# First unit of a fused state-space and feed-forward kernel: the order of the copies of the first two groups of channels, and the first product with B in quarters

## The chip, the cores and the metric

The kernel runs on one core of one Trainium2 chip. The metric is the device time of one launch in microseconds (us). The kernel before was timed three times: 323.78, 324.98 and 325.20 us, median 324.98 us.

## The reference

The input x is 4 sequences of 1024 positions with D = 128 channels, in float32. The part that matters here is the first half of a layer, a selective state-space block:

```
u  = silu(conv3(x))                       # three taps along the sequence, per channel
B, C = split(u @ W_bc + b_bc)             # 16 states each
dt = softplus((u @ W_dt + b_dt) @ W_dtp + b_dtp)
h[t, d, n] = exp(A[d, n] * dt[t, d]) * h[t-1, d, n] + B[t, n] * u'[t, d] * dt[t, d]
y[t, d]    = sum over n of C[t, n] * h[t, d, n]
x1 = layernorm(x + y + x * Dcoeff)
```

where u' is the block's own input x. The second half is a gated feed-forward layer (128 to 352 to 128) whose operands are rounded block by block to a 4-bit format, followed by another residual and layernorm. The recurrence over t is the part with most work: 128 channels by 16 states by 4096 positions.

## The kernel before

**Tiles.** The 4096 positions are cut into 8 units of 512. A unit has 128 channels x 16 states = 2048 rows of recurrence, which are handled as 16 groups of 128 partitions. A group is 32 channels (`E`) times 4 states: group k belongs to the set of states m = k // 4 and to the quarter of the channels c = k % 4. So the first four groups of a unit are the four quarters of the channels for the first set of states.

**Data of a unit.** `dtx[:, 0]` holds dt and `dtx[:, 1]` holds dt times x, with channels on the 128 partitions. Since a group has each of its 32 channels four times, once for each state, `dt_rep[:, c]` must hold quarter c of `dtx` four times over, on partitions 0-31, 32-63, 64-95 and 96-127. That is done by DMA: 4 copies of 128 KB for each quarter, 16 copies for a unit. Each quarter has its own semaphore `dt_in[c]`, complete at 64.

**Engines in the scan.** For each group ACT computes the decay `exp(A dt)` from `dt_rep[:, c, 0]` into one of three PSUM banks `ps_decay` (`decay`, L567; mean about 0.69 us). DVE multiplies `B + bias` (broadcast by PE into the bank `ps_b`, `spread_b`, L1523) with `dt_rep[:, c, 1]` into `db` (`times_b`, L1156, four quarters at once), and then runs the recurrence for a group as one scan (`scan`, L1167). POOL multiplies pairs of states with C (`times_c`, L896), and PE sums over states. C is brought onto all partitions by a PE product that ACT evacuates with a bias into `c_rep`. The engines run ahead of each other by written-out slots: step k of a unit holds decay k + 2 on ACT, scan k on DVE, the product of a pair on POOL at odd k, and pieces of the next and the previous units. A decay needs the bank that the scan of three groups before has read.

**The first unit.** It has its own head, since nothing runs beside it. `ACT` computes dt (L594), `DVE` multiplies it with x (L1133) and then prepares the quantisation of the feed-forward weights. When `dtx` is complete, ACT issues the four copies of quarter 1 (L598) and SP those of quarters 0, 2 and 3 (`replicate`, L508, called at L536). Then ACT evacuates C of set 0 (`c_of_first(0)`), loads the table set of exp and ln, evacuates C of set 1, computes decays 0 and 1 and evacuates C of set 2. PE makes each of these C products in the bank `ps_y` and may start the next one only when ACT has evacuated the one before (`c_of_first`, L1448), so the two engines take turns. After that the loop over k begins. In its first step ACT does decay 2, C of set 3, and the evacuation of the next unit's transposed x (`x_of`, L626); in its second decay 3. PE's order there is: transposes of the next unit's x, C product of set 3, the first convolution tap of the next unit (which needs `x_of`), and then `spread_b` of set 1, which needs that the product of set 0 with B is complete (`db_done`), and the other two taps.

The first product with B is made on DVE in two halves (`half_times_b`, L1146): quarters 0 and 1 in one instruction, which waits for the copies of both; then scans 0 and 1; then quarters 2 and 3 in a second instruction, then scans 2 and 3; then the product for set 1 (`times_b(s, 1, p)`, called in slot 4).

The functions that the diff touches and their callers:

Of the kernel before, what the change touches and what calls it, by code (L numbers as in the profile page):

```python
# [38 lines left out]
STATES = 4  # L39
# [145 lines left out]
def over(t, n):  # L185

    return t.rearrange("p (a t) -> p a t", a=1).broadcast_to([t.shape[0], n, t.shape[1]])


def build(nc, x, conv_w, w_bc, b_bc, w_dt, b_dt, w_dtp, b_dtp, a_log, dcoeff, w_gate, w_up, w_down, out):  # L190
# [6 lines left out]
    with ctx:  # L197
# [8 lines left out]
        def sem(name):  # L206
            return ctx.enter_context(nc.semaphore(name))
# [169 lines left out]
        conv_done = sem("conv_done")  # L377
        head_c = sem("head_c")
        head_c_done = sem("head_c_done")
        db_half = sem("db_half")  # L380
        w_magic_done = sem("w_magic_done")
        w_code_order = sem("w_code_order")
        selectors = sem("selectors")
# [82 lines left out]
        @block.sync  # L466
        def _(sp):
            def load(a, o):
                unit = a.at(1)
                if a.beyond(2):  # L470
                    sp.wait_ge(prep_mm, a.at(PREP_MM, 1 - 2 * PREP_MM))
                sp.dma_start(x_tok[o][:], x_tiles[bass.ds(unit, 1)].rearrange("a p q d -> (a p) q d"))\
                  .then_inc(x_in[o], 16)

            def load_halo(a, o):

                row = a.at(UNIT, -1 if o else UNIT)
                if a.beyond(2):
                    sp.wait_ge(sum_done, a.at(SETS, 1 - 2 * SETS))
                halo = x_feat[1][:, 0:1] if o else x_feat[0][:, UNIT + 1:UNIT + 2]  # L480
                sp.dma_start(halo, x_rows[:, bass.ds(row, 1)]).then_inc(halo_in[o], 16)

            load(Unit(0), 0)
            sp.dma_start(taps[:], conv_w.rearrange("k d -> d k")).then_inc(taps_in, 16)
            load_halo(Unit(0), 0)
            for dst, src in (
                (wdt_t, w_dt.rearrange("d r -> r d")), (wdtp, w_dtp),
                (bdt[:], b_dt.rearrange("(p a) -> p a", a=1)),
                (bdtp[:], b_dtp.rearrange("(p a) -> p a", a=1)),
            ):  # L490
                sp.dma_start(dst, src).then_inc(z_in, 16)
            for dst, src in (
                (wbc[:], w_bc), (dskip[:], dcoeff.rearrange("(p a) -> p a", a=1)),
                (bbc[:], b_bc.rearrange("(a k) -> a k", a=1).broadcast_to([128, 2 * N])),
            ):
                sp.dma_start(dst, src).then_inc(vec_in, 16)
            for i, w in enumerate((w_gate, w_up)):
                sp.dma_start(wraw[:, i * 3 * D:(i * 3 + 2) * D].rearrange("p (j d) -> p j d", d=D),
                             w[0:2 * 128, :].rearrange("(j p) d -> p j d", p=128)).then_inc(w_in, 16)
                start, rows = CHUNKS[2]  # L500
                sp.dma_start(wraw[0:rows, (i * 3 + 2) * D:(i * 3 + 3) * D],
                             w[start:start + rows, :]).then_inc(w_in, 16)
            sp.dma_start(wraw[:, 6 * D:6 * D + INNER], w_down).then_inc(w_in, 16)

            load(Unit(1), 1)
            load_halo(Unit(1), 1)

            def replicate(a, o, quarters=range(QUADS)):  # L508

                sp.wait_ge(dt_out, a.at(1, 1))  # L510
                sp.wait_ge(dtx_done, a.at(1, 1))
                for c in quarters:
                    for n in range(STATES):
                        sp.dma_start(dt_rep[o][n * E:(n + 1) * E, c], dtx[c * E:(c + 1) * E]).then_inc(dt_in[c], 16)  # L514

            def store(h, o):
                unit = h.at(1)
                sp.wait_ge(y_done, h.at(1, 1))
                sp.dma_start(out_tiles[bass.ds(unit, 1)].rearrange("a p q d -> (a p) q d"),
                             y_out[o][:].rearrange("p (q d) -> p q d", d=D)).then_inc(stored[o], 16)  # L520

            def step(b, a, s, f, g, h, p):
                if b is not None:
                    load(b, p)
                if a is not None and not s.beyond(1):
                    replicate(a, 1 - p, (0, 1))
                    load_halo(b, p)
                    replicate(a, 1 - p, (2, 3))
                elif a is not None:
                    replicate(a, 1 - p)  # L530
                if b is not None and s.beyond(1):
                    load_halo(b, p)
                if h is not None:
                    store(h, 1 - p)

            replicate(Unit(0), 0, (0, 2, 3))  # L536

            def tail(f, g, h, p):
                store(h, p)
                for i in range(2):  # L540
                    if i:
                        store(g, 1 - p)
                    sp.wait_ge(last_y, i + 1)
                    sp.dma_start(out_tiles[bass.ds(f.at(1), 1)].rearrange("a p q d -> (a p) q d")[:, 2 * i:2 * i + 2],
                                 y_out[p][:].rearrange("p (q d) -> p q d", d=D)[:, 2 * i:2 * i + 2])\
                      .then_inc(stored[p], 16)

            run(step, tail)
            for o in range(2):
                sp.wait_ge(stored[o], 16 * (UNITS // 2 + o))  # L550
# [3 lines left out]
        def _(act):  # L554
# [8 lines left out]
            def tables(which):  # L563
                act.add_instruction(mybir.InstLoadActFuncSet(  # L564
                    act_func_set_id=which, name=nc.get_next_instruction_name(), engine=mybir.EngineType.Activation))
# [11 lines left out]
            def head(a):  # L577

                act.wait_ge(prep_mm, 1)
                nc.scalar.activation(x_feat[0][:, 1:UNIT + 1], ps_prep[:], ACT.Copy).then_inc(prep_evac, PREP_EVAC)  # L580
                act.wait_ge(conv_done, 1)
                nc.scalar.activation(tanh_c[:], conv_0, ACT.Tanh).then_inc(tanh_done, 1)
                act.wait_ge(alog_in, 16 * QUADS)
                nc.scalar.activation(aexp[:].rearrange("p c k -> p (c k)"), alog[:].rearrange("p c k -> p (c k)"),
                                     ACT.Exp).then_inc(scan_ready, 1)
                act.wait_ge(scan_ready, 1)
                for n in range(STATES):
                    rows = slice(n * E, (n + 1) * E)
                    nc.scalar.activation(aneg[rows], aexp[rows].rearrange("p c (m n) -> p n c m", n=STATES)[:, n],
                                         ACT.Copy, scale=-1.0).then_inc(scan_ready, 1)  # L590
                act.wait_ge(z_ready, 2)
                nc.scalar.activation(table_in[:, 1:2], bz[:], ACT.Softplus)
                act.wait_ge(prep_mm, PREP_MM)
                nc.scalar.activation(dtx[:, 0, :], ps_prep[:], ACT.Softplus, bias=bz[:]).then_inc(dt_out, 1)  # L594
                act.wait_ge(dtx_done, 1)
                act.wait_ge(dt_out, 1)
                for n in range(STATES):
                    act.dma_start(dt_rep[0][n * E:(n + 1) * E, 1], dtx[E:2 * E]).then_inc(dt_in[1], 16)  # L598
                act.wait_ge(selectors, 1)
                c_of_first(0)  # L600
                tables(EXP_LN)
                act.wait_ge(scan_ready, 1 + STATES)
                c_of_first(1)
                for k in range(AHEAD):
                    decay(a, k, 0)
                c_of_first(2)

# [420 lines left out]
        def _(dve):  # L1028
# [114 lines left out]
                    else:  # L1143
                        last.then_inc(w_magic_done, 1)

            def half_times_b(part):  # L1146

                cs = slice(2 * part, 2 * part + 2)
                dve.wait_ge(b_mm, 1)
                for c in range(QUADS)[cs]:  # L1150
                    dve.wait_ge(dt_in[c], 16 * STATES)
                nc.vector.scalar_tensor_tensor(
                    out=db[0][:, cs], in0=over(ps_b[:], 2), scalar=bbc_rep[:, 0, 0:1], in1=dt_rep[0][:, cs, 1, :],
                    op0=ALU.add, op1=ALU.mult).then_inc(db_done if part else db_half, 1)

            def times_b(s, m, p):  # L1156
                dve.wait_ge(b_mm, s.at(SETS, m + 1))
# [9 lines left out]
            def scan(s, k, p):  # L1167
# [8 lines left out]
                elif s.beyond(2):  # L1176
                    dve.wait_ge(product_done, s.at(PAIRS, (k - ring - GROUPS) // 2 + 1))
                dve.wait_ge(decay_done, s.at(GROUPS, k + 1))
                if k < 2 and not s.beyond(1):
                    dve.wait_ge(db_half, 1)  # L1180
                else:
                    dve.wait_ge(db_done, s.at(SETS, k // QUADS + 1))
                nc.vector.tensor_tensor_scan(  # L1183
# [65 lines left out]
            def step(b, a, s, f, g, h, p):  # L1249
                first = not s.beyond(1)  # L1250
                for k in range(GROUPS):
                    if k == 2 and first:
                        half_times_b(1)
                    if k == 4 and first:
                        times_b(s, 1, p)
                    for m, slot in enumerate(AT["dve db"]):
# [163 lines left out]


            head()
            half_times_b(0)
            run(step, tail)


# [374 lines left out]
```

## Time and profile before

| | us |
|---|---|
| median of three timed runs | 324.98 |
| the profiled execution, own time | 324.9 |
| its span in the trace | 323.1 |
| DVE busy | 297.2 (92%) |
| POOL busy | 260.7 (81%) |
| PE busy | 256.0 (79%) |
| ACT busy | 244.5 (76%) |

The profile is one execution. Its own time is 324.9 us, the span that the trace covers 323.1 us; 1.8 us lie outside the span. Engines are PE (matrix), PEld (its weight loads), DVE (vector), ACT (scalar), POOL (GpSimd) and SP (the engine that issues most DMAs). A name with a q at the end (SPq, ACTq) is the engine's sequencer, which also issues DMAs. Busy shares over the whole span don't say what a change in the first 30 us is worth; for that the stretch itself has to be read.

### The profile page before, as it was taken

Reading aid. Unit: us, or ns where it says so; the run is one execution under the profiler, and the core shown is the slowest. Engines: PE = TensorE matmul, PEld = TensorE weight load, DVE = VectorE, ACT = ScalarE, POOL = GpSimd, SP = SyncE. Lnnn points to the kernel's source line nnn. Section 1 sums busy time; section 2 is a strip of 40 time slices with the busy share of each in tenths; the row PEclk is TensorE's granted clock in tenths of the full one; section 3 lists DMA queues with packets and bytes.
Section 4 is the critical chain, followed back from the end, with each engine's and each line's share of the span. In section 5 each row is a group of like instructions: output and inputs, shape, how many; then the busy total and the mean of one; then the engine's idle time right before and its main releaser. Section 6 shows DMA issues by size and latency. Waiting matters only on the chain.

```text
span 323.1 us, 3998 instructions
## 1 busy us (share of the span) xinstructions
PE 256.0 (79%) x1160; PEld 127.2 (39%) x1160; DVE 297.2 (92%) x329; ACT 244.5 (76%) x527; POOL 260.7 (81%) x146
## 2 busy tenths in 40 slices
PE   2766987658963997978897979879794869989984
PEld 1222432113421433534453335434441336536774
DVE  3778998999999999999999999999999799999873
ACT  2477789757876689698979988888888586646675
POOL 0066677578639999899999999999999997997581
PEclk9979799989997899999999999999999797999999
DMA  3691570920083002730083207410561000100003
GB/s 40 150 211 32 121 176 19 208 65 0 18 196 81 2 1 57 172 72 25 0 182 81 65 3 156 104 32 2 113 148 32 3 0 0 32 3 1 0 2 97
DMA packets 19261, 21.85 MB, mean 68 GB/s; under 512 B 6112, under 2 KB 15144, under 8 KB 19240
## 3 DMA queue, kind: packets, MB, share of 16 engines
q1 hardware_dynamic: 18520, 21.05, 28.9%
q10 hardware_dynamic: 720, 0.56, 0.9%
q8 instruction: 9, 0.15, 0.2%
q14 instruction: 12, 0.10, 0.1%
HBM read 2.72 MB, written 2.10 MB: 15 GB/s over the span
## 4 chain that ended last, share of the span: by engine, by line
POOL 43%; issue 16%; DVE 14%; PE 11%; ACT 8%; SPq 4%; DMA 2%; DVEq 0%; POOLq 0%; ACTq 0%
POOL product L905 21%; DVE states L1183 6%; POOL qh_norm L952 5%; DVE db L1163 4%; POOL qh_magic L932 4%; POOL qh_norm L927 3%; SPq L514 3%; ACT ps_decay L574 2%; POOL qx_norm L938 2%; PE ps_f L1606 2%; POOL qx_magic L932 1%; POOL qx_norm L927 1%; POOL dtx L913 1%; POOL xq L946 1%; PE ps_f L1569 1%
## 5 line engine op out<-in xcount | busy, mean ns | idle before, releaser
L905 POOL TENSOR_TENSOR product<-states,c_rep 128x1024 f32<-128x1024 f32 x59 | 128.0, 2186 | 17.7 <-DVE states L1183 17.2
L574 ACT ACTIVATE ps_decay<-dt_rep,aneg 128x512 f32<-128x512 f32 x128 | 86.8, 691 | 26.8 <-DVE states L1183 18.8
L1183 DVE TENSOR_TENSOR_SCAN states<-ps_decay,db 128x512 f32<-128x512 f32 x64 | 75.0, 1203 | 0.3
L1163 DVE SCALAR_TENSOR_TENSOR db<-ps_b,bbc_rep,dt_rep 128x2048 f32<-128x2048 f32 x31 | 72.1, 2326 | 1.6 <-PE ps_b L1527 1.6
L1183 DVE TENSOR_TENSOR_SCAN states<-ps_decay,states,db 128x512 f32<-128x512 f32 x54 | 66.6, 1261 | 1.0 <-ACT ps_decay L574 1.0
L1521 PE MATMUL ps_prep<-u_feat,wbc_rep 128*128 128x512 f32 x56 | 33.7, 685 | 11.4 <-ACT c_rep L650 11.3
L1527 PE MATMUL ps_b<-u_feat,wbc_rep 128*128 128x512 f32 x64 | 37.0, 662 | 5.4 <-DVE db L1163 4.9
L564 ACT ACT_TABLE_LOAD x26 | 33.4, 1283 | 0.5
L1485 PE MATMUL ps_y<-product,gather 128*32 128x512 f32 x248 | 32.2, 610 | 0.8 <-POOL product L905 0.8
L1569 PE MATMUL ps_f<-gate_t,xq_t 128*128 128x352 f32 x48 | 18.7, 514 | 8.4 <-ACT hidden L657 7.0
L650 ACT ACTIVATE c_rep<-ps_prep,bbc_rep 128x512 f32<-128x512 f32 x28 | 19.2, 686 | 7.0 <-PE ps_prep L1521 6.9
L1508 PE MATMUL ps_prep<-x_feat,tap_diag 128*128 128x512 f32 x42 | 19.5, 595 | 1.3 <-issue 1.3
L1521 PEld LDWEIGHTS ps_prep<-u_feat,wbc_rep 128*128 128x128 f32 x56 | 9.5, 207 | 23.9 <-ACT c_rep L650 22.5
L1527 PEld LDWEIGHTS ps_b<-u_feat,wbc_rep 128*128 128x128 f32 x64 | 10.9, 200 | 19.4 <-issue 10.0
L962 POOL TENSOR_TENSOR hq<-qh_magic,qh_scale 128x1408 f32<-128x1408 bf16 x7 | 18.1, 2586 | 0.6
L952 POOL TENSOR_TENSOR qh_norm<-hidden,qh_inv 128x1408 f32<-128x1408 f32 x7 | 18.2, 2594 | 0.0
L1606 PE MATMUL ps_f<-down_t,hq_t 128*128 128x128 f32 (+1 forms) x120 | 17.7, 286 | 0.0
L932 POOL TENSOR_TENSOR qh_magic<-qh_norm,qh_magic 128x1408 bf16<-128x1408 f32 x6 | 17.2, 2872 | 0.1
L927 POOL TENSOR_TENSOR qh_norm<-qh_norm,qh_magic 128x1408 f32<-128x1408 f32 x6 | 17.2, 2859 | 0.0
L1575 PE MATMUL ps_f<-up_t,xq_t 128*128 128x352 f32 x48 | 17.1, 479 | 0.0
L1620 PE MATMUL ps_f<-ident,hq 128*128 128x128 f32 (+1 forms) x60 | 9.5, 281 | 9.5 <-POOL hq L962 6.3
L1214 DVE TENSOR_TENSOR hidden<-hidden,ps_f 128x352 f32<-128x352 f32 x26 | 13.0, 514 | 4.4 <-PE ps_f L1575 3.9
(256 smaller groups left out, 493.0 us busy)
## 6 DMA issues: line engine op xcount, KB each, us to landing
dt_rep<-dtx SPq DMA_DIRECT2D x124, 128.0 KB, 2.4
x_tok<-in_L_attn_x SPq DMA_DIRECT2D x8, 256.0 KB, 3.1
out<-y_out SPq DMA_DIRECT2D x7, 256.0 KB, 2.3
dt_rep<-dtx ACTq DMA_DIRECT2D x4, 128.0 KB, 3.7
out<-y_out SPq DMA_DIRECT2D x2, 128.0 KB, 1.8
hidden<-in_L_ffn_w_down SPq DMA_DIRECT2D x1, 176.0 KB, 3.5
x_feat<-in_L_attn_x SPq DMA_DIRECT2D x8, 0.5 KB, 2.2
hidden<-in_L_ffn_w_gate SPq DMA_DIRECT2D x1, 128.0 KB, 2.9
```

Source lines behind the costliest of these rows:

```text
L564: act.add_instruction(mybir.InstLoadActFuncSet(act_func_set_id=which, name=nc.get_next_instruction_name(), engine=mybir.EngineType.Activat ...
L574: nc.scalar.activation(ps_decay[BANK_OF[i]][:], dt_rep[p][:, c, 0, :], ACT.Exp, scale=aneg[:, c, m:m + 1]).then_inc(decay_done, 1)
L905: nc.gpsimd.tensor_tensor(in_turn(product[:, j % PRODUCTS]), in_turn(groups(s, 2 * j, 2)), in_turn(over(c_rep[p][:, j // SET_PAIRS, :], 2) ...
L927: order.mark(nc.gpsimd.tensor_tensor(b.norm[:, 0:width], b.norm[:, 0:width], b.magic[:, 0:width], ALU.add))
L932: order.mark(nc.gpsimd.tensor_tensor(b.magic[:, 0:width], b.norm[:, 0:width], b.magic[:, 0:width], ALU.subtract))
L952: nc.gpsimd.tensor_tensor(blocked(qh.norm[:]), blocked(flat(hidden[:])), spread_out(qh.inv[:]), ALU.mult).then_inc(h_norm_done, 1)
L1163: nc.vector.scalar_tensor_tensor(out=db[m % DB][:], in0=over(ps_b[:], QUADS), scalar=bbc_rep[:, 0, m:m + 1], in1=dt_rep[p][:, :, 1, :], op ...
L1183: nc.vector.tensor_tensor_scan(out=groups(s, k, 1)[:, 0, :], data0=ps_decay[BANK_OF[s.at(GROUPS, k)]][:], data1=db[k // QUADS % DB][:, k % ...
L1485: last = nc.tensor.matmul(ps_y[c * E:(c + 1) * E, :], gather[:], product[:, (m * SET_PAIRS + c // 2) % PRODUCTS, c % 2, :], start=False, s ...
L1521: nc.tensor.matmul(ps_prep[:], wbc_rep[:, 1, m], u_feat[o][:], start=True, stop=True).then_inc(prep_mm, 1)
L1527: nc.tensor.matmul(ps_b[:], wbc_rep[:, 0, m], u_feat[o][:], start=True, stop=True).then_inc(b_mm, 1)
L1606: last = nc.tensor.matmul(bank[:, columns], hq_chunk(j, rows), down_t[0:rows, j, :], start=False, stop=(j == 2))
```

## The change

The copies of quarters 0 and 1 in the first unit are split between the two issuing engines in another way: SP issues states 0 and 2 of quarter 0, then states 0 and 2 of quarter 1; ACT issues states 1 and 3 of quarter 0, then states 1 and 3 of quarter 1. SP then issues quarters 2 and 3 as before. On ACT the table load stands right behind the DMA issues, decay 0 stands between C of set 0 and C of set 1, and decay 1 behind C of set 1. On DVE the first product with B is four instructions of 128x512 instead of two of 128x1024. Each waits for its own quarter's copies and stands right before the scan of its own group.

```diff
-            def replicate(a, o, quarters=range(QUADS)):
+            def replicate(a, o, quarters=range(QUADS), states=range(STATES)):
                 sp.wait_ge(dt_out, a.at(1, 1))
                 sp.wait_ge(dtx_done, a.at(1, 1))
                 for c in quarters:
-                    for n in range(STATES):
+                    for n in states:
                         sp.dma_start(dt_rep[o][n * E:(n + 1) * E, c], dtx[c * E:(c + 1) * E]).then_inc(dt_in[c], 16)
...
-            replicate(Unit(0), 0, (0, 2, 3))
+            replicate(Unit(0), 0, (0, 1), (0, 2))
+            replicate(Unit(0), 0, (2, 3))
...
                 nc.scalar.activation(dtx[:, 0, :], ps_prep[:], ACT.Softplus, bias=bz[:]).then_inc(dt_out, 1)
                 act.wait_ge(dtx_done, 1)
                 act.wait_ge(dt_out, 1)
-                for n in range(STATES):
-                    act.dma_start(dt_rep[0][n * E:(n + 1) * E, 1], dtx[E:2 * E]).then_inc(dt_in[1], 16)
+                for c in range(2):
+                    for n in (1, 3):
+                        act.dma_start(dt_rep[0][n * E:(n + 1) * E, c], dtx[c * E:(c + 1) * E]).then_inc(dt_in[c], 16)
+                tables(EXP_LN)
                 act.wait_ge(selectors, 1)
                 c_of_first(0)
-                tables(EXP_LN)
                 act.wait_ge(scan_ready, 1 + STATES)
+                decay(a, 0, 0)
                 c_of_first(1)
-                for k in range(AHEAD):
+                for k in range(1, AHEAD):
                     decay(a, k, 0)
                 c_of_first(2)
...
-            def half_times_b(part):
-
-                cs = slice(2 * part, 2 * part + 2)
+            def quarter_times_b(c):
+
                 dve.wait_ge(b_mm, 1)
-                for c in range(QUADS)[cs]:
-                    dve.wait_ge(dt_in[c], 16 * STATES)
+                dve.wait_ge(dt_in[c], 16 * STATES)
                 nc.vector.scalar_tensor_tensor(
-                    out=db[0][:, cs], in0=over(ps_b[:], 2), scalar=bbc_rep[:, 0, 0:1], in1=dt_rep[0][:, cs, 1, :],
-                    op0=ALU.add, op1=ALU.mult).then_inc(db_done if part else db_half, 1)
+                    out=db[0][:, c], in0=ps_b[:], scalar=bbc_rep[:, 0, 0:1], in1=dt_rep[0][:, c, 1, :],
+                    op0=ALU.add, op1=ALU.mult).then_inc(db_done if c == QUADS - 1 else db_quarter, 1)
...
                 dve.wait_ge(decay_done, s.at(GROUPS, k + 1))
-                if k < 2 and not s.beyond(1):
-                    dve.wait_ge(db_half, 1)
+                if k < QUADS - 1 and not s.beyond(1):
+                    dve.wait_ge(db_quarter, k + 1)
                 else:
                     dve.wait_ge(db_done, s.at(SETS, k // QUADS + 1))
...
                 for k in range(GROUPS):
-                    if k == 2 and first:
-                        half_times_b(1)
+                    if 0 < k < QUADS and first:
+                        quarter_times_b(k)
                     if k == 4 and first:
                         times_b(s, 1, p)
...
             head()
-            half_times_b(0)
+            quarter_times_b(0)
             run(step, tail)
```

## Rows read from the trace of the kernel before

**Rows 1.** The page: span, shares of the chain by engine.

```profile
span 323.1 us, 3998 instructions
...
POOL 43%; issue 16%; DVE 14%; PE 11%; ACT 8%; SPq 4%; DMA 2%; DVEq 0%; POOLq 0%; ACTq 0%
```

**Rows 2.** Chain of waits in order of time, 12 to 60: start, us, what.

```profile
13.74 0.83 SPq L514
...
22.18 2.65 DMA dt_rep<-dtx
...
28.68 2.25 DVE db L1163
```

**Rows 3.** Timeline of DVE: start, us, instructions, in brackets idle time before, releaser.

```profile
17.86 0.45 DVE L1119 TENSOR_SCALAR qh_magic<-qh_magic 128x1120 bf16<-128x1120 bf16 x1
20.47 1.28 DVE L1152 SCALAR_TENSOR_TENSOR db<-ps_b,bbc_rep,dt_rep 128x1024 f32<-128x1024 f32 x1 [2.15 <-DMA dt_rep<-dtx]
21.86 2.34 DVE L1183 TENSOR_TENSOR_SCAN states<-ps_decay,db 128x512 f32<-128x512 f32 x2
24.95 1.28 DVE L1152 SCALAR_TENSOR_TENSOR db<-ps_b,bbc_rep,dt_rep 128x1024 f32<-128x1024 f32 x1 [0.76 <-DMA dt_rep<-dtx]
26.34 2.34 DVE L1183 TENSOR_TENSOR_SCAN states<-ps_decay,db 128x512 f32<-128x512 f32 x2
28.60 2.33 DVE L1163 SCALAR_TENSOR_TENSOR db<-ps_b,bbc_rep,dt_rep 128x2048 f32<-128x2048 f32 x1
```

**Rows 4.** DMA issues between 13.9 and 14.2: KB each, us to landing.

```profile
dt_rep<-dtx ACTq DMA_DIRECT2D x1, 128.0 KB, 3.1
dt_rep<-dtx SPq DMA_DIRECT2D x1, 128.0 KB, 4.3
```

**Rows 5.** Timeline of ACT, 12 to 36.

```profile
13.04 3.24 ACTq L598 DMA_DIRECT2D dt_rep<-dtx  x4
16.39 0.69 ACT L610 ACTIVATE c_rep<-ps_y,bbc_rep 128x512 f32<-128x512 f32 x1 [4.10 <-PE ps_y L1451]
17.09 1.28 ACT L564 ACT_TABLE_LOAD   x1
18.39 0.69 ACT L610 ACTIVATE c_rep<-ps_y,bbc_rep 128x512 f32<-128x512 f32 x1
20.39 1.30 ACT L574 ACTIVATE ps_decay<-dt_rep,aneg 128x512 f32<-128x512 f32 x2 [1.32 <-DMA dt_rep<-dtx]
...
22.67 0.69 ACT L574 ACTIVATE ps_decay<-dt_rep,aneg 128x512 f32<-128x512 f32 x1 [0.37 <-DMA dt_rep<-dtx]
23.52 0.69 ACT L610 ACTIVATE c_rep<-ps_y,bbc_rep 128x512 f32<-128x512 f32 x1 [0.15 <-PE ps_y L1451]
24.10 0.59 ACT L631 ACTIVATE x_feat<-ps_prep 128x512 f32<-128x512 f32 x1
24.86 1.30 ACT L574 ACTIVATE ps_decay<-dt_rep,aneg 128x512 f32<-128x512 f32 x2 [0.16 <-DMA dt_rep<-dtx]
```

**Rows 6.** Timeline of PE, 14 to 48.

```profile
17.12 1.12 PE L1451 MATMUL ps_y<-u_feat,wbc_rep 128*128 128x512 f32 x2 [1.70 <-ACT c_rep L610]
19.12 2.07 PE L1451 MATMUL ps_y<-u_feat,wbc_rep 128*128 128x512 f32 x2 [0.88 <-ACT c_rep L610]
...
24.80 1.10 PE L1508 MATMUL ps_prep<-x_feat,tap_diag 128*128 128x512 f32 x2 [1.31 <-issue]
26.29 1.13 PE L1527 MATMUL ps_b<-u_feat,wbc_rep 128*128 128x512 f32 x2 [0.40 <-DVE db L1152]
```

**Rows 7.** Windows: stretch, length, busy PE, PEld, DVE, ACT, POOL, clock, DMA, GB/s.

```profile
16.50:18.50 2.00, 1.12 (x2) 0.30 (x2) 1.74 (x3) 1.97 (x3) 0.03 (x1) 1.00 0.98 197
19.00:22.00 3.00, 2.88 (x6) 1.38 (x6) 1.43 (x2) 1.68 (x4) 2.92 (x2) 0.50 0.96 238
22.50:25.00 2.50, 1.19 (x3) 0.39 (x4) 1.74 (x3) 2.02 (x4) 2.42 (x2) 1.00 0.85 193
...
28.60:50.00 21.40, 17.40 (x64) 6.86 (x62) 21.30 (x16) 18.32 (x28) 14.03 (x7) 0.92 0.50 112
```

More of the change, by code:

```diff
@@ L379, in build @@
         head_c_done = sem("head_c_done")
-        db_half = sem("db_half")
+        db_quarter = sem("db_quarter")
         w_magic_done = sem("w_magic_done")
```

## The prediction

> **What bounds the kernel now.** I read the page first. Over the whole span of 323.1 us the chain is mostly POOL's [rows 1], but the change touches only the first 30 us, so the page's shares say nothing of its worth; what they say is that nothing but the work itself sets the rest. Second, the chain of waits in order of time: up to 24.83 it runs through SP's copy issues into the last copy of the unit, issued at 22.18 and landed 2.65 later, and from there through DVE's first product to the product for set 1, where it stays on DVE [rows 2]. Third, the timeline of DVE in that stretch [rows 3]: it is free at 18.31, idles to 20.47 for the copies of quarters 0 and 1, multiplies for 1.28, scans groups 0 and 1 to 24.20, idles again for the last copies, and only from 24.95 on does it do the second half (1.28), scans 2 and 3 (2.34), and at 28.60 the product for set 1. Fourth, a window from 28.60 to 50: DVE is busy 21.30 of 21.40 us [rows 7]. So DVE is the bound from 28.60 on, and the start of the product for set 1, 28.60, is the number to watch: I expect what it moves by to be the change in the whole time. After that stretch every wait of the chain is for another engine's work or for a copy that such work released; no input from outside arrives late, so the shift is carried to the end whole. I take it at 1.0 of the shift; the bound below is that it fades.
>
> **The change part by part.**
>
> *Product with B in quarters.* 128x1024 takes 1.28 and 128x2048 takes 2.33, so 1024 columns more cost 1.05 and a quarter of 512 columns costs 1.28 - 0.52 = 0.76 [rows 3]. Four of them are 3.04 against 2.56: 0.48 more on DVE. Three of them lie in its idle time before 24.95. After the last copy (24.83) there remain one quarter (0.76) and one scan in place of 1.28 and two scans. A pair of scans takes 2.34, and its first one half of that, 1.17. The gain is 0.52 + 1.17 = 1.69, less what is late instead. If nothing is late, quarter 3 ends at 24.95 + 0.76 = 25.71, scan 3 starts at 25.82 (0.11 later, as at 26.34) and the product for set 1 at 28.60 - 1.69 = 26.91. That product also needs PE's product for set 1: it started 0.06 after the half ended and took 1.13 [rows 6], now 25.77 to 26.90. So 26.95 is the earliest, a gain of 1.65. This is the upper end.
>
> *Copies.* The number of copies on each queue, their sizes and total stay. The second issue of each queue landed 3.1 and 4.3 us after issue [rows 4]; SP's was issued at 13.74 [rows 2], so at 18.04, and ACT's, the second of four from 13.04 on [rows 5], at about 16.8. These four places now hold quarter 0: it is complete at 18.04, where before both quarters had landed only at 20.4, when DVE and ACT resume together [rows 3, 5]. Bounds for quarter 0: 16.8, if the queues even out, and 20.4, if the eight copies finish together. I take 18.04, since it is the very place in the queue. Quarters 1, 2 and 3 keep theirs: 20.4, 22.6 (decay 2 starts at 22.67, released by a copy) and 24.83.
>
> *ACT's order, and the turns between PE and ACT for C.* This is the part that costs. ACT's issues end at 16.28. Before, C of set 0 was evacuated at 16.39 and the load (1.28) ran behind it while PE made the next product [rows 5, 6]. Now the load goes first: 16.30 to 17.58, C of set 0 17.60 to 18.29, so PE starts the product for set 1 at 18.33 in place of 17.12. Since quarter 0 landed at 18.04, decay 0 runs 18.30 to 18.99, hidden behind PE. Two C products follow. A pair of matmuls took 1.12 in a stretch whose granted clock was 1.00 (2.4 GHz) and 2.07 where it was 0.50 (1.2 GHz) [rows 6, 7]. The clock fell at about 18.7 after PE had been idle 1.70 us before 17.12 and short of work behind it, and came back at about 22.1. With that same course:
> - C of set 1 on PE: 30% done at 18.67, the rest 0.7 x 2.07 = 1.45, end 20.12. ACT evacuates 20.16 to 20.85.
> - C of set 2 on PE from 20.89, slow until 22.1, end 22.56. ACT has done decay 1 by 21.55 and evacuates 22.60 to 23.29.
> - C of set 3 on PE, behind it and the transposes, 23.33 to 24.45. ACT does decay 2, 23.30 to 23.99, evacuates C 24.49 to 25.18, then x (0.59, overlapping 0.1) to 25.67, then decay 3, 25.68 to 26.37. Before, these were at 23.52, 24.10 and 24.86 [rows 5].
> - PE's first tap starts 0.11 after x, 25.78, and the product with B for set 1 stands behind it on PE: 0.97 for a pair that follows another without a gap (26.29 to 27.26, where its next taps start), so 26.75 to 27.85.
> - DVE: quarter 0 at 18.40, scan 0 19.2 to 20.4, quarter 1 to 21.2, scan 1 behind decay 1, 21.6 to 22.8, quarter 2 to 23.6, scan 2 behind decay 2, 24.05 to 25.25, quarter 3 to 26.0, scan 3 behind decay 3, 26.45 to 27.65, and the product for set 1 behind PE at 27.9.
>
> So 28.60 becomes 27.9: of the 1.65 some 0.95 is given back, and the wait that ends last there is PE's product for set 1 (`spread_b`), just ahead of it decay 3. ACT's later window follows decay 6, which needs scan 3, so it is early by about the same 0.9, and DVE's work up to 50 hides it.
>
> *What the pages would make of it.* The load ended at 18.37 and the next evacuation began at 18.39 [rows 5], so in this trace nothing but the 1.28 is paid. The Trainium skill, ScalarE: Activation LUTs, "What ACT_TABLE_LOAD costs", has a drain of about 1.38 us with each switch of tables, 2.66 together; by it, as an estimate, C of set 0 and all behind it come 1.38 later than above, and the kernel is about 0.7 us slower, 325.6. The rows decide against that, and no term rests on it.
>
> **The sum.** Profiled execution: 324.9 - 0.7 = 324.2. The median of the runs shown is 324.98, 0.1 above that execution, so I forecast 324.2 for either.
>
> **The rivals.**
> 1. *Full gain.* The C products meet the clock at 1.00, each pair 1.12: C of set 1 ends 19.45, of set 2 at 21.3, of set 3 at 23.2, and decay 3 stays at 24.86. Then 26.95 holds: 1.65 less, 323.3. For it: the three timed runs lie 1.4 us apart, so such courses differ. Against it: PE is now idle for longer, 2.9 us instead of 1.70 before the C product of set 1. The Trainium skill, TensorE: Matmul & The Clock Gate, "What's actually happening", says that the slow clock is the default and activity lifts it, and that the matmuls it hits vary from run to run; the granted clock here agrees with the first (0.50 after the idle time), no run here shows the second.
> 2. *Quarter 0 is not early.* The eight copies share the DMA engines (share 0.98 and 0.96 [rows 7]) and finish near 20.4 together. Then decay 0 holds ACT to 21.1, C of set 1 is evacuated to 21.8, C of set 2 is on PE to about 23.0, of set 3 24.5 to 25.6, x done at 26.8, decay 3 at 27.5, and the product for set 1 at 28.6: no gain, 324.9. Against it: the second issues landed well before the fourth.
> 3. *The other side: slower.* The clock, lower for longer since PE has less to do up to 22, stays at 0.50 through the C product of set 3. Then C of set 2 ends 22.96, of set 3 goes 23.85 to 25.92, x is done at 27.1, decay 3 at 27.8, PE's tap 27.2 to 28.3, and its product for set 1 at 29.3: 0.7 slower, 325.6; with the tap at that clock as well 1 to 2 us more, 327. It decides once that product ends after 28.5. For it: PE was busy 2.88 of 3.00 us in the low stretch before [rows 7], and has some 0.3 less there now. Against it: 22.5 to 25 ran at 1.00 with only 1.19 of 2.50 busy.
> 4. *The shift fades.* The 0.7 is gained at 28.60 and lost in a PE stretch later: 324.9. Nothing in the rows speaks for it.
>
> **How the numbers follow.** The forecast (gain 0.3 to 1.2) has a chance of 0.47, full gain 0.25, quarter 0 late 0.08, slower 0.13, fading 0.07. The range 322.9 to 325.6 holds the forecast, the full gain with some spread below 323.3, rivals 2 and 4, and slower up to its mild form; it leaves out about 0.15. The forecast's own range is 323.6 to 324.7. Within 0.5%, that is 1.6 us, a measurement of this kernel can't be told from no change. Faster by more than that needs the full gain and luck: 0.21. Slower by more needs rival 3 in its hard form: 0.07. Same: 0.72.
>
> **What would show it.** In the changed trace: the first DVE product near 18.4 and a first decay near 18.3 (else rival 2); DVE's product for set 1 near 27.9 (26.95: rival 1; past 28.6: rival 3), with PE's `ps_b` as its releaser; C evacuations at 17.6, 20.2, 22.6 and 24.5; decay 3 at 25.7; four products with B of 0.76 us. If the start of the product for set 1 moves by 0.7 or more and the whole time by less than half of that, the carrying is what failed.

## The result, and the profile after

Over all timed runs the changed kernel takes 325.82 us in the median of 18 (324.73 to 328.04), the kernel before 324.90 (323.78 to 326.04). The ratio is 1.0029, interval 1.0017 to 1.0042: 0.9 us slower, less than the 0.5% named in the forecast and yet clear of zero. Forecast was 324.2, with a range from 322.9 to 325.6. The profiled execution is among the longer ones of its kernel: its own time is 327.06, its span 325.3.

The page after: span, busy time, chain by engine.

```profile
span 325.3 us, 4003 instructions
...
PE 260.1 (80%) x1160; PEld 127.3 (39%) x1160; DVE 297.9 (92%) x331; ACT 244.5 (75%) x527; POOL 260.8 (80%) x146
...
POOL 38%; DVE 19%; issue 18%; PE 12%; ACT 8%; SPq 1%; ACTq 1%; DMA 1%; DVEq 0%; POOLq 0%
```

DVE's work has grown by only 0.7, ACT's not at all and POOL's by 0.1. SP's copy issues have left the chain (4% of it in [rows 1], now 1%), and PE has 12% in place of 11%. The timeline of DVE after:

```profile
18.20 0.75 DVE L1153 SCALAR_TENSOR_TENSOR db<-ps_b,bbc_rep,dt_rep 128x512 f32<-128x512 f32 x1
...
20.62 0.75 DVE L1153 SCALAR_TENSOR_TENSOR db<-ps_b,bbc_rep,dt_rep 128x512 f32<-128x512 f32 x1 [0.34 <-DMA dt_rep<-dtx]
...
25.15 0.75 DVE L1153 SCALAR_TENSOR_TENSOR db<-ps_b,bbc_rep,dt_rep 128x512 f32<-128x512 f32 x1 [0.31 <-DMA dt_rep<-dtx]
26.96 1.22 DVE L1184 TENSOR_TENSOR_SCAN states<-ps_decay,db 128x512 f32<-128x512 f32 x1 [1.06 <-ACT ps_decay L575]
30.05 2.35 DVE L1164 SCALAR_TENSOR_TENSOR db<-ps_b,bbc_rep,dt_rep 128x2048 f32<-128x2048 f32 x1 [1.87 <-PE ps_b L1528]
```

"Product for set 1" is below always DVE's product of 128x2048, and its start is the number that the prediction watched. Against [rows 3] the first three quarters do what they were meant to: the first starts as DVE comes free, and only one quarter and one scan are left after the last copy. But scan 3 waits 1.06 for its decay, and the product for set 1 then 1.87 for PE. It starts at 30.05, where it was at 28.60. ACT and PE show why; timeline of ACT, then of PE, after:

```profile
16.27 1.28 ACT L565 ACT_TABLE_LOAD   x1 [4.00 <-issue]
17.56 0.69 ACT L613 ACTIVATE c_rep<-ps_y,bbc_rep 128x512 f32<-128x512 f32 x1
...
19.46 0.69 ACT L613 ACTIVATE c_rep<-ps_y,bbc_rep 128x512 f32<-128x512 f32 x1 [0.61 <-PE ps_y L1452]
...
22.32 0.69 ACT L613 ACTIVATE c_rep<-ps_y,bbc_rep 128x512 f32<-128x512 f32 x1 [1.08 <-PE ps_y L1452]
...
25.17 0.69 ACT L613 ACTIVATE c_rep<-ps_y,bbc_rep 128x512 f32<-128x512 f32 x1 [1.58 <-PE ps_y L1452]
25.75 0.59 ACT L634 ACTIVATE x_feat<-ps_prep 128x512 f32<-128x512 f32 x1
26.23 2.68 ACT L575 ACTIVATE ps_decay<-dt_rep,aneg 128x512 f32<-128x512 f32 x4
```

```profile
18.30 1.13 PE L1452 MATMUL ps_y<-u_feat,wbc_rep 128*128 128x512 f32 x2 [2.92 <-ACT c_rep L613]
20.20 2.07 PE L1452 MATMUL ps_y<-u_feat,wbc_rep 128*128 128x512 f32 x2 [0.78 <-ACT c_rep L613]
...
23.06 2.08 PE L1452 MATMUL ps_y<-u_feat,wbc_rep 128*128 128x512 f32 x2
26.45 2.05 PE L1509 MATMUL ps_prep<-x_feat,tap_diag 128*128 128x512 f32 x2 [1.31 <-issue]
28.28 1.73 PE L1528 MATMUL ps_b<-u_feat,wbc_rep 128*128 128x512 f32 x2
```

One product of the program shows as two MATMULs in the trace, a pair. PE idles 2.92 us before the C product of set 1, 1.70 before [rows 6]. That pair is still fast (1.13). From the next on each takes 2.05 to 2.08, and the product with B 1.73, since the clock comes back within it; it ends at 30.0. The granted clock in windows after (third from the end of each row, ahead of DMA share and GB/s):

```profile
16.00:19.00 3.00, 0.70 (x2) 0.30 (x2) 2.88 (x4) 2.57 (x3) 0.56 (x1) 1.00 0.99 193
19.00:22.00 3.00, 2.22 (x3) 0.73 (x3) 2.50 (x3) 1.38 (x2) 2.92 (x2) 0.57 0.96 239
22.00:26.00 4.00, 3.13 (x7) 1.15 (x5) 3.42 (x4) 2.10 (x4) 3.92 (x3) 0.50 0.77 178
26.00:29.00 3.00, 2.56 (x3) 1.17 (x4) 1.22 (x1) 2.91 (x6) 2.17 (x2) 0.50 0.00 0
30.00:33.00 3.00, 2.31 (x7) 0.77 (x6) 2.85 (x2) 1.43 (x3) 0.42 (x1) 1.00 0.00 0
```

Before, the clock was back at 1.00 in 22.5 to 25 [rows 7]. Here it stays at 0.50 (1.2 GHz) from 19.4 to 29.7. Of the 2.2 us between the two spans 1.45 are there at this one start. The lag stays near that up to DVE's product with B at 49.31 (47.83 before) and is 2.26 at the next, at 58.11 (55.85). Between them, from 54 to 56, this trace has the clock at 0.50 and that of before at 1.00. That this second low stretch makes the other 0.8 is not tested.

### The profile page after: what moved, and what is told of

It reads as the page before. It is cut to its first block, busy times and chain, and to the rows that moved or that the text cites. A ratio compares the mean times of both kernels' runs of the same rounds, so it can differ in the third digit from the quotient of the medians.

```text
span 325.3 us, 4003 instructions
## 1 busy us (share of the span) xinstructions
PE 260.1 (80%) x1160; PEld 127.3 (39%) x1160; DVE 297.9 (92%) x331; ACT 244.5 (75%) x527; POOL 260.8 (80%) x146
## 4 chain that ended last, share of the span: by engine, by line
POOL 38%; DVE 19%; issue 18%; PE 12%; ACT 8%; SPq 1%; ACTq 1%; DMA 1%; DVEq 0%; POOLq 0%
POOL product L908 18%; DVE states L1184 7%; DVE db L1164 7%; POOL qh_norm L955 5%; POOL qh_magic L935 4%; POOL qh_norm L930 3%; ACT ps_decay L575 2%; DVE dt_rep L1184 2%; POOL qx_norm L941 2%; PE ps_y L1452 2%; PE ps_f L1576 1%; POOL dtx L916 1%; PE ps_f L1570 1%; POOL qx_magic L935 1%; POOL qx_norm L930 1%
## 5 line engine op out<-in xcount | busy, mean ns | idle before, releaser
L575 ACT ACTIVATE ps_decay<-dt_rep,aneg 128x512 f32<-128x512 f32 x128 | 86.9, 691 | 25.1 <-DVE states L1184 19.4
L1486 PE MATMUL ps_y<-product,gather 128*32 128x512 f32 x248 | 33.1, 625 | 0.3 <-POOL product L908 0.3
L1570 PE MATMUL ps_f<-gate_t,xq_t 128*128 128x352 f32 x48 | 19.9, 543 | 7.7 <-ACT hidden L660 5.7
L653 ACT ACTIVATE c_rep<-ps_prep,bbc_rep 128x512 f32<-128x512 f32 x28 | 19.2, 686 | 4.6 <-PE ps_prep L1522 4.4
L1509 PE MATMUL ps_prep<-x_feat,tap_diag 128*128 128x512 f32 x42 | 20.4, 619 | 2.1 <-issue 2.1
L965 POOL TENSOR_TENSOR hq<-qh_magic,qh_scale 128x1408 f32<-128x1408 bf16 x7 | 18.1, 2586 | 0.6
L1576 PE MATMUL ps_f<-up_t,xq_t 128*128 128x352 f32 x48 | 18.1, 505 | 0.0
L1522 PEld LDWEIGHTS ps_prep<-u_feat,wbc_rep 128*128 128x128 f32 x56 | 9.2, 200 | 22.0 <-ACT c_rep L653 20.6
L1570 PEld LDWEIGHTS ps_f<-gate_t,xq_t 128*128 128x128 f32 x48 | 9.1, 211 | 21.0 <-ACT hidden L660 10.9
```

Source lines behind the costliest of these rows:

```text
L575: nc.scalar.activation(ps_decay[BANK_OF[i]][:], dt_rep[p][:, c, 0, :], ACT.Exp, scale=aneg[:, c, m:m + 1]).then_inc(decay_done, 1)
L1486: last = nc.tensor.matmul(ps_y[c * E:(c + 1) * E, :], gather[:], product[:, (m * SET_PAIRS + c // 2) % PRODUCTS, c % 2, :], start=False, s ...
L1522: nc.tensor.matmul(ps_prep[:], wbc_rep[:, 1, m], u_feat[o][:], start=True, stop=True).then_inc(prep_mm, 1)
L1570: nc.tensor.matmul((ps_f1, ps_f2)[i % 2][:, 0:INNER], xq_t[:, i * 128:(i + 1) * 128], gate_t[:], start=True, stop=True).then_inc(gate_mm, 1)
```

## The experiments

Theory A: the load ahead of C of set 0 leaves PE idle, its clock stays low through the turns for C, and PE's product with B for set 1 is late. Theory B: the split copies or the smaller DVE products cost the time. The runs came in three groups, e1 to e4, e5 to e8 and e9 to e12, each on one chip and beside the kernel before; every ratio is against those runs of before.

**e1: ACT's order as before.**

```diff
+                act.wait_ge(selectors, 1)
+                c_of_first(0)
                 tables(EXP_LN)
-                act.wait_ge(selectors, 1)
-                c_of_first(0)
                 act.wait_ge(scan_ready, 1 + STATES)
-                decay(a, 0, 0)
                 c_of_first(1)
-                for k in range(1, AHEAD):
+                for k in range(AHEAD):
                     decay(a, k, 0)
```

> The changed kernel with ACT's order of before: the table load behind C of set 0, decays 0 and 1 behind C of set 1. Copies and quarters stay changed. Theory A (the load ahead of C of set 0 leaves PE idle, the granted clock stays at 0.50 through PE's next products, and the product with B for set 1 is late): the C product of set 1 starts near 17.1 again, the clock is back at 1.00 near 22, the product for set 1 on DVE starts near 26.95, and the kernel is 1.0 to 1.7 us faster than before. Theory B (the split copies or the four smaller DVE products cost the time): still slower than before, about as the changed kernel, +0.9.

Measured: 324.73 (323.25 to 324.97), ratio 0.9983 (0.9968 to 0.9998). The loss is gone and B falls. But the gain is 0.15 us by the medians and 0.55 by the ratio, where 1.0 to 1.7 was expected: five of the twelve runs lie at 323.2 to 324.0, seven at 324.7 to 325.0. The profile is one of the seven and shows where the gain went in it; PE, then DVE:

```profile
24.80 1.84 PE L1508 MATMUL ps_prep<-x_feat,tap_diag 128*128 128x512 f32 x2 [1.58 <-issue]
26.44 1.92 PE L1527 MATMUL ps_b<-u_feat,wbc_rep 128*128 128x512 f32 x2
```

```profile
28.39 2.35 DVE L1163 SCALAR_TENSOR_TENSOR db<-ps_b,bbc_rep,dt_rep 128x2048 f32<-128x2048 f32 x1 [1.03 <-PE ps_b L1527]
```

In this execution the clock was at 1.00 through all the turns and low at 25.0 to 28.4 instead, and it hit the tap and the product with B. With DVE early, that product has no slack any more: whatever slows PE just there is paid.

**e2: ACT's new order alone**, in the kernel before (the reverse of the diff above).

> The kernel before with ACT's new order alone: load ahead of C of set 0, decay 0 ahead of C of set 1; copies and the two halves as before. Theory A: slower than before by 1 to 3 us, since decay 0 waits for its copies until 20.4 and holds C of set 1 as well; the product for set 1 on DVE starts between 29.5 and 31.5. Theory B: within 0.3 us of before.

Measured: 326.52 (324.91 to 328.44), ratio 1.0057 (1.0035 to 1.0079), and the product for set 1 at 31.70, 0.2 past the expectation. As A had it: ACT's order costs in the old kernel too, and more without the early copies, since decay 0 then waits until 20.48 and C of set 1 behind it until 21.11.

**e3: the changed kernel with PE kept busy.**

```diff
+                for _ in range((0, 3, 0, 0)[m]):
+                    nc.tensor.matmul(ps_f2[:], wz[:], u_feat[0][:], start=True, stop=True)
                 if m:
                     pe.wait_ge(head_c_done, m)
                 nc.tensor.matmul(ps_y[:], wbc_rep[:, 1, m], u_feat[0][:], start=True, stop=True).then_inc(head_c, 1)
+                if m == 3:
+                    for _ in range(1):
+                        nc.tensor.matmul(ps_f2[:], wz[:], u_feat[0][:], start=True, stop=True)
```

> The changed kernel with four extra products on PE into a bank that nothing reads, three between the C products of sets 0 and 1 and one behind that of set 3. They only keep PE busy. Theory A with the clock as the cause: granted clock 1.00 from 18 to 29, C of set 3 evacuated near 23.3, the product for set 1 on DVE near 26.95, 1.65 us faster than before. Theory A without the clock (it is ACT's order alone that makes the turns late): the start moves by less than 0.3 from that of the changed kernel, still slower. Theory B: no difference from the changed kernel.

Measured: 323.83 (322.47 to 324.98), ratio 0.9964 (0.9948 to 0.9981). Nothing but idle time on PE was filled, and the kernel went from 0.9 slower to 1.1 faster than before, where 1.65 was expected. Windows, then DVE:

```profile
19.00:22.00 3.00, 2.09 (x8) 0.80 (x6) 2.50 (x4) 1.91 (x3) 2.92 (x2) 1.00 0.97 238
22.00:26.00 4.00, 3.08 (x6) 0.98 (x6) 3.50 (x4) 2.79 (x6) 3.92 (x3) 1.00 0.78 182
26.00:29.00 3.00, 2.84 (x6) 1.05 (x6) 2.92 (x2) 2.71 (x4) 3.00 (x2) 1.00 0.00 0
```

```profile
27.22 2.33 DVE L1164 SCALAR_TENSOR_TENSOR db<-ps_b,bbc_rep,dt_rep 128x2048 f32<-128x2048 f32 x1
```

The clock is 1.00 throughout, the C pairs take 1.13 (1.02 behind an extra one), C of set 3 is evacuated at 23.41, and the product for set 1 waits for nobody. So in the changed order it is the clock that makes the turns late, not the order as such.

**e4: the changed kernel again.**

> The changed kernel once more, on the same chip as the other three. All theories: 0.9 us slower than before in the median, single runs from 324.7 to 328. Theory A: the mean granted clock of a run goes with its time, lower clock, longer time; the profile's start of the product for set 1 lies between 27 and 30 and follows the clock between 19 and 29.

Measured: 325.74 (324.77 to 327.99), ratio 1.0037 (1.0013 to 1.006). Its profile has the clock low from 17.0 to 30.7 and the product for set 1 at 31.02, outside my 27 to 30, with a span of 326.2:

```profile
31.02 2.35 DVE L1164 SCALAR_TENSOR_TENSOR db<-ps_b,bbc_rep,dt_rep 128x2048 f32<-128x2048 f32 x1 [1.89 <-PE ps_b L1528]
```

The mean clock goes with the time only roughly: the three slowest runs have 0.939 to 0.945, the four fastest 0.955 to 0.967.

**e5: only the load moved back**, behind `c_of_first(0)`; decay 0 stays ahead of C of set 1.

> The changed kernel with the table load alone moved back behind C of set 0; decay 0 stays ahead of C of set 1. It separates the two edits of ACT's order. Theory A (the load ahead of C of set 0 opens PE's gap): PE's idle time before the C product of set 1 is 1.7 to 1.9 again instead of 2.9, and the time is that of the kernel with all of ACT's order as before, 324.7 (323.3 to 325.0). Rival: decay 0 ahead of C of set 1 is what makes the turns late: still near 325.8.

Measured: 323.77 (323.22 to 326.49), ratio 0.9988 (0.997 to 1.0007). By the medians that is 1.0 below before, and better than the 324.7 expected, which was the time of e1. Eight of twelve runs lie below 324.1, none of the 30 of the changed kernel with its order whole does. So the load is the larger part of the loss. Two runs at 325.3 and 326.5 keep the ratio from being clear of 1. PE in its profile:

```profile
17.14 1.13 PE L1452 MATMUL ps_y<-u_feat,wbc_rep 128*128 128x512 f32 x2 [1.49 <-ACT c_rep L613]
19.75 2.08 PE L1452 MATMUL ps_y<-u_feat,wbc_rep 128*128 128x512 f32 x2 [1.48 <-ACT c_rep L613]
...
22.60 1.13 PE L1452 MATMUL ps_y<-u_feat,wbc_rep 128*128 128x512 f32 x2
```

The gap before the first of these pairs is 1.49. The clock is low from 19.2 to 22.6 and comes back 0.5 later than forecast for the changed kernel, just as C of set 3 begins, which is fast. The product for set 1 starts at 27.23.

**e6: the kernel before with PE kept busy**, three extra products as in e3, ahead of sets 1 and 3 and behind set 3.

> The kernel before with three extra products on PE into a bank that nothing reads (one ahead of the C product of set 1, one ahead of and one behind that of set 3). Control for the run with PE kept busy: in the kernel before, DVE sets the start of the product for set 1 (28.60) and not PE, so the theory expects that start within 0.2 of 28.60 and a time within 0.5 us of before. Rival (a warmer clock is worth as much in any order, through the stretches after 30 us): 1 us faster than before, as the run with PE kept busy was.

Measured: 325.05 (324.53 to 326.52), ratio 1.0013 (1.0001 to 1.0025): with the clock at 1.00 from 14 to 34, nothing is gained in the order of before. The start was at 29.04, 0.2 outside the expectation; in that execution DVE's first half was at 20.79 already, 0.32 later than in [rows 3].

**e7: quarters alone**, copies and ACT's order as before.

> The kernel before with the product with B in quarters and nothing else: copies and ACT's order as before. Quarter 0 is complete only at 20.4, so DVE does four products and four scans in a row from there: 20.45 + 4 x 0.75 + 4 x 1.2 + gaps 0.2 = 28.4 for the product for set 1, a gain of 0.2 to 0.3. Expected time 324.6, within 0.3 us of before. If it is as fast as the kernel with split copies at full clock (-1 or more), the split of the copies was worth nothing.

Measured: 324.64 (324.24 to 325.07), ratio 0.9995 (0.9985 to 1.0005). DVE from 20.45 on:

```profile
20.45 0.75 DVE L1150 SCALAR_TENSOR_TENSOR db<-ps_b,bbc_rep,dt_rep 128x512 f32<-128x512 f32 x1 [2.14 <-DMA dt_rep<-dtx]
...
28.35 2.33 DVE L1161 SCALAR_TENSOR_TENSOR db<-ps_b,bbc_rep,dt_rep 128x2048 f32<-128x2048 f32 x1
```

Four products and four scans in a row fill that time, as worked out. The split of the copies is what lets the first quarter and its scan go ahead of 20.4. Its worth shows in e1, which differs from this run in the copies alone: there DVE was ready at 27.36 (28.39 less its wait of 1.03 for PE), 1.0 earlier. In e5, where PE is in time, the start is 1.1 earlier, but that kernel has decay 0 ahead of C of set 1 as well.

This profile has the clock low from 17.3 to 24.2, though ACT's order is that of before. PE, then ACT:

```profile
17.11 1.87 PE L1449 MATMUL ps_y<-u_feat,wbc_rep 128*128 128x512 f32 x2 [2.35 <-ACT c_rep L610]
22.67 1.86 PE L1449 MATMUL ps_y<-u_feat,wbc_rep 128*128 128x512 f32 x2
```

```profile
24.56 0.69 ACT L610 ACTIVATE c_rep<-ps_y,bbc_rep 128x512 f32<-128x512 f32 x1 [1.21 <-PE ps_y L1449]
```

All three C pairs are slow here too, but the turns began at 17.11, and DVE doesn't wait for them.

**e8: the product with B ahead of the next unit's first tap**, in the changed kernel.

```diff
-    "pe x": 0, "pe conv": (1, 2), "pe z": 3, "pe C": (7, 9, 10, 11), "act x": 0, "act window": 4,
+    "pe x": 0, "pe conv": (2,), "pe z": 3, "pe C": (7, 9, 10, 11), "act x": 0, "act window": 4,
```

> The changed kernel with one edit in PE's order: the product with B for set 1 stands ahead of the next unit's first tap, and the three taps follow in one place. If the theory names the last wait rightly (that product behind the tap, behind x, behind C of set 3), it no longer waits for x: it starts when quarter 3 is done (26.0 in the profile of the changed kernel) and ends at 27 to 28.1, and DVE's product for set 1 starts when scan 3 ends, 28.2 in that profile, instead of 30.05. Time 1 to 1.8 us below the changed kernel, 324.0 to 324.9. Against: the taps end up to 1 us later, so ACT's window is later; if that decides, no gain over the changed kernel.

Measured: 325.14 (324.08 to 326.0), ratio 1.001 (0.9996 to 1.0024), about 0.6 below the changed kernel, less than the 1 to 1.8 expected. Its profile has the clock low from 18.1 to 24.9:

```profile
27.39 1.22 DVE L1184 TENSOR_TENSOR_SCAN states<-ps_decay,db 128x512 f32<-128x512 f32 x1 [0.96 <-ACT ps_decay L575]
28.52 2.33 DVE L1164 SCALAR_TENSOR_TENSOR db<-ps_b,bbc_rep,dt_rep 128x2048 f32<-128x2048 f32 x1
```

The wait for PE is gone and the one before it decides, the decay behind the late C of set 3. Both hang on the same turns.

**e11, e12: two more profiles of the changed kernel.**

> The changed kernel, one look. Open is what its runs near 324.8 look like (8 of 18 there, where the forecast's course gave 324.2 and the profiled run was 327.1). Theory: the start of the product for set 1 plus 294.5 to 295.2 gives the span in every one; a run of 324.8 (span 323.0) has it near 28.2, with PE's pairs slow for C of sets 1 to 2 or 3, and fast again for the product with B.

> The same kernel, a second look, for another course of the clock. Same expectation: span less the start of the product for set 1 between 294.3 and 295.3.

Measured: 324.71 and 324.76, spans 322.9 and 323.0, the start at 28.80 and 28.67. Both miss the 28.2 expected by some 0.5; span less start is 294.1 and 294.3, the first below what was expected. The clock is low from 18.0 to 24.8 and from 17.7 to 24.5. e11, PE and then DVE:

```profile
18.29 2.07 PE L1452 MATMUL ps_y<-u_feat,wbc_rep 128*128 128x512 f32 x2 [3.12 <-ACT c_rep L613]
21.14 2.08 PE L1452 MATMUL ps_y<-u_feat,wbc_rep 128*128 128x512 f32 x2 [0.78 <-ACT c_rep L613]
...
23.99 1.50 PE L1452 MATMUL ps_y<-u_feat,wbc_rep 128*128 128x512 f32 x2
26.81 1.10 PE L1509 MATMUL ps_prep<-x_feat,tap_diag 128*128 128x512 f32 x2 [1.31 <-issue]
27.74 1.02 PE L1528 MATMUL ps_b<-u_feat,wbc_rep 128*128 128x512 f32 x2
```

```profile
28.80 2.35 DVE L1164 SCALAR_TENSOR_TENSOR db<-ps_b,bbc_rep,dt_rep 128x2048 f32<-128x2048 f32 x1 [0.26 <-PE ps_b L1528]
```

Even the better of the two courses seen for this kernel has two C pairs slow and a third in part, and that eats the whole gain.

**e9: load behind C of set 0, and PE kept busy** (extra products `(0, 1, 1, 0)[m]` ahead of the C products and one behind that of set 3).

> The changed kernel with the table load behind C of set 0, and with three extra products on PE into a bank that nothing reads (ahead of the C products of sets 1 and 2 and behind that of set 3), so that both losses are removed at once. By the theory (time outside the start of the product for set 1 is 294.5 to 295.2 in span, and that start is 27.2 when PE's pairs take 1.1): median 323.3, 1.5 us below before, and the runs above 325 of the kernel with the load moved back alone are gone. Rival: the spread of single runs comes from after 30 us, then it stays.

Measured: 323.31 (322.50 to 323.87), ratio 0.9954 (0.9935 to 0.9972). It beats both kernels: 1.6 us below before in the medians of that group, and its slowest run is below the fastest of before (324.31) there. Its start is the earliest of all:

```profile
24.99 0.75 DVE L1153 SCALAR_TENSOR_TENSOR db<-ps_b,bbc_rep,dt_rep 128x512 f32<-128x512 f32 x1 [0.16 <-DMA dt_rep<-dtx]
25.84 1.22 DVE L1184 TENSOR_TENSOR_SCAN states<-ps_decay,db 128x512 f32<-128x512 f32 x1
26.98 2.33 DVE L1164 SCALAR_TENSOR_TENSOR db<-ps_b,bbc_rep,dt_rep 128x2048 f32<-128x2048 f32 x1
```

**e10: e9 with the edit of e8**, two extra products behind C of set 3.

> As the run before, and with PE's product with B for set 1 ahead of the next unit's first tap (two extra products behind C of set 3 in place of one). With PE at full clock that product isn't last: it waits for quarter 3 either way. So the theory expects no difference from the run before, within 0.3 us; a slower one would mean that the later taps cost.

Measured: 323.25 (322.99 to 323.86), ratio 0.9956 (0.9941 to 0.997): no difference, as expected.

Over all fourteen profiles (span, start of the product for set 1, difference):

| kernel | start | span | difference |
|---|---|---|---|
| before | 28.60 | 323.1 | 294.5 |
| changed (four profiles) | 30.05, 31.02, 28.80, 28.67 | 325.3, 326.2, 322.9, 323.0 | 295.2, 295.2, 294.1, 294.3 |
| e1, e2, e3 | 28.39, 31.70, 27.22 | 323.1, 326.6, 321.5 | 294.7, 294.9, 294.3 |
| e5, e6, e7, e8 | 27.23, 29.04, 28.35, 28.52 | 321.4, 323.0, 322.8, 323.3 | 294.2, 294.0, 294.4, 294.8 |
| e9, e10 | 26.98, 27.22 | 321.1, 321.6 | 294.1, 294.4 |

## Why the prediction was wrong

*The number to watch, and that it is carried.* Right in the main. The starts spread over 4.7 us, what follows over 1.2. Starts a us or more apart order the spans; the seven between 28.35 and 29.04 have spans of 322.8 to 323.3 in no order, so what follows isn't constant either. "The shift fades" (rival 4) is out.

*Quarters.* Right: 0.76 forecast, 0.75 measured for each; DVE has 0.7 more in all, where 0.48 was forecast.

*Copies.* Right: quarter 0 was there when DVE came free, at 18.20 at the latest, against 18.04 forecast, and ACT's decay 0 ran at 18.16; "quarter 0 is not early" (rival 2) is out. Quarter 1 came at 20.6 and quarter 3 was multiplied at 25.15, each 0.2 later than forecast.

*ACT's order.* Right up to PE's start of the C product of set 1: 18.33 forecast, 18.30 measured. The wait that ends last is the one named, PE's `spread_b`, behind the tap, x and C of set 3.

*The step that failed* is the clock's course: it "came back at about 22.1. With that same course", C of set 2 was to end at 22.56 and C of set 3, the tap and the product with B to run at full clock, to 27.85. I took the times at which the clock fell and rose from the trace of before and laid them under a schedule in which PE idles for longer. In all four profiles of the changed kernel it stayed low for longer than that: to 24.5 and 24.8 (e12, e11), to 29.7 and 30.7 (the first profile, e4). By the first course the C pairs of sets 1 and 2 are wholly slow and that of set 3 in part (1.35 and 1.50 in place of 1.12), so C of set 3 is evacuated at 25.40 and 25.54 where 24.49 was forecast, and the start is 28.7 to 28.8 in place of 27.9. By the second C of set 3 (2.08), the tap (2.05 in place of 1.10) and the product with B (1.73 in place of 1.10) are slow, and the start is 30.05 to 31.0. In the first profile the clock fell only at 19.4, so that C of set 2 was evacuated at 22.32, 0.3 ahead of the forecast: all of the loss there stands behind the moment at which I had let the clock rise. The 0.7 gain thus became nothing or a loss. That is the side of rival 3, priced at 29.3 and up, with a chance of 0.13 where it should have had the larger share. What I held against it, that 22.5 to 25 ran at 1.00 with little work, was a row of a stretch before which PE had been busier.

Is it the longer idle time that keeps the clock low? e3 shows that filling it removes the low stretch and the loss. e5, with a gap of 1.5 in place of 2.9 to 3.6, has a short low stretch and most of the loss is gone, but there the turns also begin 1.2 earlier, so that the same low stretch would cost less. The two are not separated. With the load ahead of C of set 0 and PE not kept busy, the recorded low stretches in the turns are 7 to 14 us long (the changed kernel and e8). With it behind they are 3 to 4 us (before, e1, e5) and 7 (e7), so the order of before can meet a long one too. That the load's place lengthens the low stretch is likely by these rows and not shown.

*Full gain* (rival 1) was priced nearly right: 26.95 and 323.3 forecast. In e3, the changed order with PE kept busy, it is 27.22 and 323.83; in e9, with the load moved back too, 26.98 and 323.31. The changed kernel by itself never gets there, with 324.71 as the shortest of its 32 runs.

*The pages.* The load's drain in the Trainium skill, ScalarE: Activation LUTs, "What ACT_TABLE_LOAD costs", doesn't show: in the changed kernel as well the load ends at 17.55 and C is evacuated from 17.56. The kernel was slower, but not by that. The Trainium skill, TensorE: Matmul & The Clock Gate, "What's actually happening", has activity releasing the slow clock, and the trace agrees: with PE's idle time filled (e3) it reads 1.00 from 14 to 34. The same section has the slow products vary from run to run, and that is shown now: one and the same kernel had the clock low from 18.0 to 24.8, 19.4 to 29.7 and 17.0 to 30.7.

## What to carry to other kernels

A stretch in which PE and another engine take turns is priced with PE at both of its clocks, never with the clock's course of another schedule: an edit that shifts PE's work or lets it idle longer meets another course, and each product on the path then costs 2.07 us in place of 1.13. Before work is taken off the path of one engine, look at which product stands just behind it with no slack; there a small instruction moved ahead of PE's releaser (here one table load) can cost more than the waits removed. Take several profiles of such a kernel: here the low stretch was 7 us long in one execution and 14 in another. Spare products into an unused bank are a cheap test of this, and here they were also the cure.

## What the runs showed of the hardware

One 128x512 product (a pair of MATMULs) takes 1.13 us at the clock's upper level, 1.02 behind another product, and 2.07 at the lower, and there is hardly anything between but where the clock changes within. The granted clock of a trace can lack a low stretch: in e2's profile it reads 1.00 from 14 to 33 while the pairs take 2.08. PE and its windows there:

```profile
21.83 2.08 PE L1452 MATMUL ps_y<-u_feat,wbc_rep 128*128 128x512 f32 x2 [1.36 <-ACT c_rep L611]
```

```profile
22.00:26.00 4.00, 4.00 (x8) 1.72 (x8) 3.16 (x3) 1.63 (x3) 3.92 (x3) 1.00 0.76 178
```

The duration of a known instruction is the safer witness of the two.
